# A layer of attention and a mixture of experts on one core: both batches routed in one run, the weight marks on ScalarE, the second half turned inside the first

## The chip, the core and the metric

The kernel runs on one core of a Trainium2 chip. A core has four compute engines with a queue each: TensorE (PE; its weight loads are listed as PEld), VectorE (DVE), ScalarE (ACT) and GpSimd (POOL); SyncE (SP) only issues transfers. The engines run on their own and meet at semaphores. All of them work from SBUF, an on-chip memory of 128 partitions; TensorE writes to PSUM. The metric is the time of the whole program on the device in microseconds; less is better. All times are from the profile of one execution or from the runs in the table below.

## What is computed

The input is 2 batches of 2048 tokens of 256 numbers. First comes attention with 16 heads of 16, added to the input and normalised; then every token goes to its two likeliest of 8 experts, the result is added and normalised again:

```
x = layernorm(x + attention(x))
probs = softmax(x @ router_weight.T)              # 4096 tokens x 8 experts
topk_probs, selected = top_k(probs, 2); weights divided by their sum
# each expert takes at most 1280 tokens, the heaviest weights first
expert_inputs[e, slot] = x[token]
expert_out = (pre * silu(gate)) @ post            # pre, gate: 256 -> 1024, post: 1024 -> 256
out[token] = sum over its kept slots of weight * expert_out
x = layernorm(x + out)
```

In this data no expert is over its 1280 places, so slots may be given in token order; the other case is in the code behind a branch and is not taken.

## The kernel before

The program is three blocks with a barrier of all engines between them. The first makes the projections and the second the attention, up to 1094 us of the span. The third holds the rest, and the change lies in it alone.

**Normalising and logits.** Tokens lie 128 to a tile, 32 tiles (`TT`), 16 (`NT`) to a batch. `measure_h(b)` on VectorE turns the row statistics of a batch into mean and scale: seven small instructions in `layer_stats` (L153 to L159), a root on ScalarE (L1289), six more. Then groups of 4 tiles are normalised in `x_sb` by VectorE and ScalarE, turned by TensorE (L1136), multiplied by the router's weights (L1144), copied by ScalarE (L1312) and turned back (L1151) into the logits `lg_ps[b]`; there are 8 groups, 4 a batch. SyncE stores the normalised rows to DRAM twice, as `h_dram` (what experts gather) and as `acc_dram` (what results are added to).

**Routing.** `route(b)` on VectorE is a chain of about 50 instructions over 16 tiles x 8 experts (128 elements): softmax (with an Exp on ScalarE, L1305), the two picks, weights, then a running count per expert (`prefixes`, from two products on TensorE, L1119 and L1120) and the place of each choice (`places`), split into a partition `at_p` and a column `at_q` of the slot table. Batch 1 adds the totals of batch 0. Each instruction waits for the one before.

**The slot table** `list_ps` (80 columns of token numbers, 80 of weights) is a sum of products. A piece `n` is one choice `k` of 8 tiles; there are 8 pieces. For a piece VectorE makes `in_q` (L1469), `in_p` (L1470) and the number marks (L1474), GpSimd makes the weight marks from `in_q` and `kept_w` (L1036), and TensorE adds up 8 fp32 products (L1160, 16 instructions). `in_q`, `in_p` and `marks` have two buffers each, so piece n+2 waits for the products of piece n (`list_ready`). VectorE copies the table out (L1598, L1599).

**Experts.** GpSimd gathers the rows of an expert from `h_dram` with ten indirect transfers: four for the first half of its slots (`xin_loaded`), six for the second half and the spare tiles (`xrest_loaded`). `turn(j, g)` on TensorE (L1194, 8 instructions) turns half `g` of 512 slots into `xt_ps`; ScalarE and VectorE copy it as a high and a low part (`turn_hi` L1276, `turn_lo` L1613; `xt_split` counts two for each half). An expert's body then has, for each half `g`, eight steps `f` of `up` (12 products of 128x512, L1202), each followed by a gate on ScalarE (L1374), the product `mid` (L1687), and its high (L1377) and low part (L1616); then eight steps of `down` (12 products of 128x256, L1210). `up(f)` waits for the `mid` of f-2. `split_down` parts the second weight matrix (high part on GpSimd L1027, low part on VectorE L1607, at `f == 4` of half 0), `split_up` the first (ScalarE L1285, VectorE L1512). Experts 0 to 5 are a loop of three rounds of two; a spare third part of 256 slots is computed only where an expert has over 1024 tokens (three of the eight). In the second half's `down` steps TensorE turns both halves of the next expert, at f = 0 and f = 4; before expert 0 both are turned as soon as their gathers have landed.

At the start of the third block GpSimd clears `y` and `xin` of both buffers (L1021, L1022: 128x2560 each), then parts expert 0's second matrix (L1027), which SyncE has loaded.

## Time and profile before

| | us |
|---|---|
| median of 3 runs (lowest, highest) | 1867.17 (1865.07, 1868.34) |
| the profiled execution: its own time | 1867.23 |
| the profiled execution: span of the trace | 1865.3 |

| stretch of the span | us |
|---|---|
| projections and attention | 0 to 1094 |
| normalising and logits | 1094 to 1148 |
| routing and slot table (overlaps the logits of batch 1) | 1138 to 1209 |
| gathering and turning for expert 0 | 1209 to 1228 |
| the eight experts | 1228 to 1834 |
| last rows out | 1834 to 1865 |

TensorE is busy in 89% of the span, ScalarE in 68%, VectorE in 64%, GpSimd in 17%. These are averages over stages that have little in common: in the stretch from 1094 to 1228 us TensorE is mostly idle, in the experts it is nearly always at work. The views used below are the page's slices (the span in 40 equal parts), the instructions in order of time, the chain of waits (what released what, back from the end), the busy time by stretch, and the groups of instructions by form.

### The profile page before, as it was taken

To read this page: it belongs to the slowest core of one execution; us is meant where nothing else is said; L and a number is where in the kernel's file an instruction comes from. 1 tells how busy PE (TensorE), PEld (TensorE's weight loads), DVE (VectorE), ACT (ScalarE), POOL (GpSimd) and SP (SyncE) were. 2 spreads that over 40 slices of the span, in tenths; PEclk is the share of its full clock that TensorE was granted. 3 is DMA by queue.
4 is the path that set the end of the run, shared out by engine and by line. 5 is a ranking of instruction groups with operands and counts; after the bars stand their busy time and mean duration, and the time that the engine had idled before them with its cause. 6 is when DMAs were issued, how large, how long until landed. Compare 5 with 4: busy or idle time off the path is not lost. (4 is left out here: it accounts for less than half of the span.)

```text
span 1865.3 us, 31730 instructions
## 1 busy us (share of the span) xinstructions
PE 1658.0 (89%) x10822; PEld 1016.4 (54%) x10823; DVE 1193.3 (64%) x2238; ACT 1271.8 (68%) x1422; POOL 323.0 (17%) x306
## 2 busy tenths in 40 slices
PE   7949999999999999999999956379989998999995
PEld 6713333333333333333333323368978997889985
DVE  6846868676777768686877766834444553545564
ACT  7739999999999999999999953023333342433433
POOL 0000000000000000000000021243424424344154
PEclk9969999999999999999999978779999999999998
DMA  5561010101010100101010005122222313323143
GB/s 176 170 183 47 30 29 23 32 19 34 17 34 17 34 24 27 28 23 32 20 34 17 17 23 180 46 68 63 61 59 60 102 14 103 68 58 101 13 124 112
DMA packets 74746, 108.27 MB, mean 58 GB/s; under 512 B 10778, under 2 KB 59715, under 8 KB 74672
## 3 DMA queue, kind: packets, MB, share of 16 engines
q1 hardware_dynamic: 59792, 89.42, 15.1%
q0 software_dynamic: 14880, 17.82, 5.5%
q8 instruction: 51, 0.84, 0.2%
q14 instruction: 23, 0.19, 0.0%
HBM read 75.77 MB, written 35.91 MB: 60 GB/s over the span
## 5 line engine op out<-in xcount | busy, mean ns | idle before, releaser
L690 ACT ACTIVATE probs<-scores 128x1536 f32<-128x1536 f32 (+1 forms) x384 | 520.6, 1379 | 42.8 <-PE scores L620 37.5
L733 DVE TENSOR_REDUCE sums<-expq 128x1 f32<-128x1408 f32 (+6 forms) x448 | 347.4, 828 | 13.0 <-ACT expq L696 13.0
L620 PE MATMUL scores<-aq,ak 98*128 98x512 bf16 (+3 forms) x1280 | 304.0, 352 | 56.9 <-DMA aq<-shift_dram 22.0
L636 PE MATMUL o_ps<-probs,vh 128*32 128x512 f32 (+3 forms) x2560 | 339.1, 542 | 0.0
L1374 ACT ACTIVATE gate<-up_ps 128x512 f32<-128x512 f32 x128 | 76.5, 598 | 327.2 <-PE up_ps L1202 327.2
L620 PE MATMUL scores<-ak,aq 98*128 98x512 bf16 (+3 forms) x1184 | 263.8, 342 | 17.0 <-ACT probs L690 9.0
L696 ACT ACTIVATE expq<-scores 128x1536 f32<-128x1536 f32 x192 | 274.7, 1449 | 2.0
L720 DVE TENSOR_TENSOR hidden<-probs,after 128x384 f32<-128x384 f32 x128 | 70.9, 554 | 238.9 <-ACT probs L690 238.9
L620 PEld LDWEIGHTS scores<-aq,ak 98*128 98x128 bf16 x1280 | 96.6, 98 | 230.2 <-ACT probs L690 73.2
L620 PEld LDWEIGHTS scores<-ak,aq 98*128 98x128 bf16 x1184 | 91.0, 98 | 238.5 <-ACT expq L696 94.7
L1202 PE MATMUL up_ps<-xeT_hi,wup_hi 128*128 128x512 f32 x512 | 203.1, 397 | 18.3 <-issue 13.5
L1687 DVE TENSOR_TENSOR mid<-up_ps,gate 128x512 f32<-128x512 f32 x128 | 88.3, 691 | 194.7 <-ACT gate L1374 192.1
L1202 PE MATMUL up_ps<-xeT_hi,wup_lo 128*128 128x512 f32 x512 | 201.6, 394 | 0.0
L1202 PE MATMUL up_ps<-xeT_lo,wup_hi 128*128 128x512 f32 x512 | 201.4, 393 | 0.0
L699 ACT ACTIVATE scores<-scores 128x1536 f32<-128x1536 f32 x128 | 185.5, 1450 | 0.0
L1210 PE MATMUL y_ps<-w_hi,mid_hi 128*128 128x256 f32 x560 | 157.3, 281 | 0.0
L1210 PE MATMUL y_ps<-w_lo,mid_hi 128*128 128x256 f32 x560 | 156.2, 279 | 0.0
L1210 PE MATMUL y_ps<-w_hi,mid_lo 128*128 128x256 f32 x560 | 156.0, 279 | 0.0
L577 POOL COPY vh<-v_all 128x256 f32 (+1 forms) x32 | 12.6, 396 | 727.5 <-PE o_ps L636 724.4
L1094 POOL DMA_INDIRECT acc_dram<-y,row x70 | 109.2, 1559 | 136.7 <-DVE y L1648 90.6
L1202 PEld LDWEIGHTS up_ps<-xeT_hi,wup_hi 128*128 128x128 f32 x512 | 97.8, 191 | 39.7 <-issue 16.0
L636 PEld LDWEIGHTS o_ps<-probs,vh 128*32 128x32 f32 x2560 | 50.8, 108 | 123.8 <-issue 98.4
(241 smaller groups left out, 2607.7 us busy)
## 6 DMA issues: line engine op xcount, KB each, us to landing
raw<-w_T SPq DMA_DIRECT2D x16, 1024.0 KB, 7.4
split_dram<-parts SPq DMA_DIRECT2D x48, 256.0 KB, 2.9
aq<-split_dram SPq DMA_DIRECT2D x192, 64.0 KB
raw<-wg_T SPq DMA_DIRECT2D x8, 1024.0 KB, 4.9
ak<-split_dram SPq DMA_DIRECT2D x32, 192.0 KB
xT<-x_T SPq DMA_DIRECT2D x8, 512.0 KB, 4.9
ak<-split_dram SPq DMA_DIRECT2D x32, 128.0 KB
x_sb<-x_tok SPq DMA_DIRECT2D x1, 4096.0 KB, 25.2
```

What stands on the lines that cost most here:

```text
L620: last = nc.tensor.matmul(dst[:, at:at + w], still, moving[0:KS, lo:lo + w], start=True, stop=True, skip_group_check=True)
L636: last = nc.tensor.matmul(dst[32 * r:32 * r + 32, BLK - w:BLK], vh[j % 2][:, k, :], probs[:, m % P_RING, at:at + w], start=first, stop=Tru ...
L690: last = nc.scalar.activation(probs[:, m % P_RING, 0:w], src[:, 0:w], ACT.Exp, scale=HD ** -0.5)
L696: last = nc.scalar.activation(expq[:, n % X_RING, 0:w], src[:, 0:w], ACT.Exp, scale=HD ** -0.5)
L699: last = nc.scalar.activation(src[:, at:at + w], src[:, at:at + w], ACT.Exp, scale=HD ** -0.5, accum_out=sums[:, j, col:col + 1])
L720: nc.vector.tensor_tensor(hidden[:, 0:3, :], three, after[:, 0:3, :], ALU.mult).then_inc(hidden_ready, 1)
L733: last = nc.vector.tensor_reduce(sums[:, j % 2, col:col + 1], expq[:, n % X_RING, at:at + w], AX.X, ALU.add)
L1094: pool.indirect_dma_start(out=acc_dram[:, :], out_offset=bass.IndirectOffsetOnAxis(ap=row[j][:, t:t + 1], axis=0), in_=y[j][:, t, :], in_o ...
L1202: last = nc.tensor.matmul(up_ps[n % 2][:, k, 0:cols.stop - cols.start], wup[a][:, k, c, f * P:(f + 1) * P], x[b][:, c, cols], start=(c == ...
L1210: last = nc.tensor.matmul(y_ps[:, t, :], mid2[a][:, f, t * P:(t + 1) * P], w2[b][:, f, :], start=(f == 0 and t % 2 == 0 and (a, b) == PAIR ...
L1374: nc.scalar.activation(gate[f % 2][:], up_ps[f % 2][:, 0, :], ACT.Silu).then_inc(silu_done, 1)
L1687: nc.vector.tensor_tensor(mid[f % 2][:], up_ps[f % 2][:, 1, :], gate[f % 2][:], ALU.mult).then_inc(mul_done, 1)
```

## The change

1. `route()` handles all 32 tiles in one run (256 elements an instruction); only the first two instructions stay per batch. One Exp on ScalarE takes both batches. The prefix products are one pair of 256 columns.
2. `split_up(0, 0)` stands before `route()`; it was between the marks of batch 0 and the routing of batch 1. The eight pieces follow in one row, ordered by tiles and then choice. The instructions on totals (L1530 to L1539 before) stand once before them, as they did before the last four.
3. The weight marks are made by ScalarE, in 8 instructions of 128x80 a piece, not by GpSimd in one of 128x640.
4. GpSimd clears only the spare part of each `y` (two instructions of 128x512).
5. Half 1 of an expert is turned inside half 0 of the same expert, before the `up` of f = 4, for expert 0 too. `split_down` moves from f = 4 to f = 5 on VectorE.

VectorE around the first stretch of routing. `wup_lo` is the low part of expert 0's first matrix, `red` and `work` are the first two steps of the routing, `rprobs` the output of the Exp. Before:

```order
L1416 TENSOR_SCALAR x_sb<-x_sb,mean,rstd 128x256 x8
L1481 TENSOR_REDUCE red<-xt_ps 128x16
L1482 TENSOR_TENSOR work<-xt_ps,red 128x128
L1485 TENSOR_REDUCE red<-rprobs 128x16
L1486 RECIPROCAL tmp<-red 128x16
```

Now:

```order
L1410 TENSOR_SCALAR x_sb<-x_sb,mean,rstd 128x256 x8
L1503 TENSOR_TENSOR wup_lo<-raw,wup_hi 128x1024 x4
L1476 TENSOR_REDUCE red<-xt_ps 128x16
L1477 TENSOR_TENSOR work<-xt_ps,red 128x128
L1476 TENSOR_REDUCE red<-xt_ps 128x16
L1477 TENSOR_TENSOR work<-xt_ps,red 128x128
L1481 TENSOR_REDUCE red<-rprobs 128x32
```

The four `wup_lo` moved ahead of the routing, and the chain behind the Exp waits for the logits of both batches.

ScalarE from the last groups of logits to the first expert. `hT` and `lT` are its copies in the logits, `xeT_hi` the high part of a turned half. Before:

```order
L1294 ACTIVATE x_sb<-x_sb,nbias,rstd 128x256 x2
L1301 ACTIVATE hT<-up_ps 128x512 x2
L1312 ACTIVATE lT<-up_ps 8x512
L1305 ACT_TABLE_LOAD
L1305 ACTIVATE rprobs<-work 128x128
L1301 ACTIVATE hT<-up_ps 128x512 x2
L1312 ACTIVATE lT<-up_ps 8x512 x2
L1305 ACTIVATE rprobs<-work 128x128
L1276 ACTIVATE xeT_hi<-xt_ps 128x512 x4
```

Now:

```order
L1282 ACTIVATE x_sb<-x_sb,nbias,rstd 128x256 x2
L1289 ACTIVATE hT<-up_ps 128x512 x2
L1305 ACTIVATE lT<-up_ps 8x512
L1289 ACTIVATE hT<-up_ps 128x512 x2
L1305 ACTIVATE lT<-up_ps 8x512 x2
L1322 ACT_TABLE_LOAD
L1322 ACTIVATE rprobs<-work 128x256
L1297 ACTIVATE marks<-in_q,kept_w 128x80 x64
L1264 ACTIVATE xeT_hi<-xt_ps 128x512 x2
```

The table load for the Exp stands behind the last copy of logits, 64 marks are new, and two of the four copies of the turned rows have gone from here.

TensorE from the end of the slot table to expert 0. Before:

```order
L1160 MATMUL y_ps<-marks,in_p 128x160 x64
L1178 UNCONDITIONAL_BRANCH
L1194 MATMUL xt_ps<-ident,xin 128x128 x16
L957 UNCONDITIONAL_BRANCH
L957 ISA
L966 TENSOR_LOAD more
```

Now, first the same place and then, behind the line of three dots, the fourth and fifth `up` of half 0:

```order
L1153 MATMUL y_ps<-marks,in_p 128x160 x64
L1170 UNCONDITIONAL_BRANCH
L1186 MATMUL xt_ps<-ident,xin 128x128 x8
L958 UNCONDITIONAL_BRANCH
...
L1194 MATMUL up_ps<-xeT_lo,wup_hi 128x512
L1230 ISA
L1186 MATMUL xt_ps<-ident,xin 128x128 x8
L1233 REGISTER_ALU
L1194 MATMUL up_ps<-xeT_hi,wup_hi 128x512
```

Eight of the sixteen turning instructions went from ahead of expert 0 to the middle of its first half.

```diff
-        PIECES = [(b, k, half) for b in range(B) for half in range(2) for k in range(TOPK)]
+        PIECES = [(k, part) for part in range(TT // OHP) for k in range(TOPK)]
+        TURN_AT_F = 4
...
                 for j in range(2):
-                    pool.memset(y[j][:], 0.0).then_inc(y_cleared, 1)
-                    pool.memset(xin[j][:], 0.0).then_inc(y_cleared, 1)
+                    pool.memset(y[j][:, 2 * NA:CT, :], 0.0).then_inc(y_cleared, 1)
...
-                for n in range(NP):
-                    k, tiles = of_piece(n)
-                    pool.wait_ge(eq_ready, n + 1)
-                    if n >= 2:
-                        pool.wait_ge(list_ready, n - 1)
-                    nc.gpsimd.tensor_tensor(marks[n % 2][:, :, 1, :], in_q[n % 2][:], wide(kept_w[:, k, tiles], NSLOT), ALU.mult).then_inc(wgt_ready, 1)
...
-                        pe.wait_ge(wgt_ready, n + 1)
+                        pe.wait_ge(wgt_ready, OHP * (n + 1))
...
-                for b in range(B):
-                    pe.wait_ge(keep_ready, b + 1)
-                    prefix_products(of_batch(b)).then_inc(prefix_ready, 1)
-                    for n in range(b * NP // B, (b + 1) * NP // B):
-                        list_piece(n, 0)
+                pe.wait_ge(keep_ready, 1)
+                prefix_products(ALL).then_inc(prefix_ready, 1)
+                for n in range(NP):
+                    list_piece(n, 0)
...
                 pe.wait_ge(xin_loaded[0], 16 * NA)
-                for g in range(2):
-                    if g == 1:
-                        pe.wait_ge(xrest_loaded[0], 16 * (CT - NA))
-                        pe.wait_ge(xt_split, DC)
-                    turn(0, g)
+                turn(0, 0)
...
-                    pe.wait_ge(xt_split, count(4, i, j, 4))
+                    pe.wait_ge(xt_split, count(4, i, j, 2))
...
                         for f in range(FC):
+                            if g == 0 and f == TURN_AT_F:
+                                pe.wait_ge(xrest_loaded[j], i * (16 * (CT - NA)) + 16 * (CT - NA))
+                                turn(j, 1)
...
                         if g == 0:
+                            pe.wait_ge(xt_split, count(4, i, j, 4))
...
-                            if g == 1 and prep and f == FC // 2:
-                                pe.wait_ge(xrest_loaded[1 - j], i * (16 * (CT - NA)) + 16 * (CT - NA) * (j + 1))
-                                pe.wait_ge(xt_split, count(2 * DC, i, j, 3 * DC))
-                                turn(1 - j, 1)
...
-                def exponentials(b):
-                    act.wait_ge(logit_off, b + 1)
-                    nc.scalar.activation(probs[:, of_batch(b), :], work[:, of_batch(b), :], ACT.Exp).then_inc(p_exp, 1)
+                def weights(n):
+                    k, tiles = of_piece(n)
+                    act.wait_ge(eq_ready, n + 1)
+                    if n >= 2:
+                        act.wait_ge(list_ready, n - 1)
+                    for t in range(OHP):
+                        nc.scalar.activation(marks[n % 2][:, t, 1, :], in_q[n % 2][:, t, :], ACT.Copy,
+                                             scale=kept_w[:, k, tiles.start + t:tiles.start + t + 1]).then_inc(wgt_ready, 1)
...
-                route(0)
-                for n in range(NP // B):
-                    mark(n, 0)
                 split_up(0, 0)
-                route(1)
+                route()
...
-                for n in range(NP // B, NP):
+                dve.wait_ge(places_ready, 1)
+                for n in range(NP):
                     mark(n, 0)
...
-                            if g == 0 and f == FC // 2:
+                            if g == 0 and f == TURN_AT_F:
+                                turn_lo(i, j, 1)
+                            if g == 0 and f == TURN_AT_F + 1:
                                 split_down(i, j)
...
                         if g == 1 and prep:
                             turn_lo(i, j + 1, 0)
                             split_up(i, j + 1)
-                            turn_lo(i, j + 1, 1)
```

## Rows read from the trace of the kernel before

**Rows 1.** Chain of waits, 1095 to 1106 us: start, duration, what.

```profile
1095.85 8.97 DVE var L158
1104.84 1.82 DVE var L159
```

**Rows 2.** GpSimd in order of time: start, duration, what.

```profile
1096.04 2.23 POOL L1021 MEMSET y<- 128x2560 f32 x1
...
1104.73 1.88 POOL L1027 CAST w_hi<-raw 128x2048 fp32r<-128x2048 f32 x1
```

**Rows 3.** By stretch: length, busy us of each engine, clock, DMA share, GB/s.

```profile
1100.00:1101.00 1.00, 0.00 (x0) 0.00 (x0) 1.00 (x1) 0.00 (x0) 1.00 (x2) 0.50 0.05 14
```

**Rows 4.** TensorE and ScalarE in order of time, the end of the logits.

```profile
1147.54 0.41 PE L1151 MATMUL xt_ps<-ident,lT 8*128 8x8 f32 x4 [0.34 <-ACT lT L1312]
...
1141.70 1.28 ACT L1305 ACT_TABLE_LOAD   x1
...
1146.90 0.59 ACT L1312 ACTIVATE lT<-up_ps 8x512 f32<-8x512 f32 x1 [1.57 <-PE up_ps L1144]
```

**Rows 5.** VectorE in order of time, the routing.

```profile
1137.80 0.29 DVE L1481 TENSOR_REDUCE red<-xt_ps 128x16 f32<-128x128 f32 x1 [6.69 <-PE xt_ps L1151]
1143.41 0.28 DVE L1485 TENSOR_REDUCE red<-rprobs 128x16 f32<-128x128 f32 x1 [4.99 <-ACT rprobs L1305]
1155.56 0.83 DVE L1469 TENSOR_TENSOR in_q<-upward,at_q 128x640 f32<-128x640 f32 x1
1171.33 4.62 DVE L1512 TENSOR_TENSOR wup_lo<-raw,wup_hi 128x1024 fp32r<-128x1024 f32 x4
1189.40 0.16 DVE L1530 TENSOR_SCALAR big<-total 1x8 f32<-1x8 f32 x1
1190.89 0.82 DVE L1469 TENSOR_TENSOR in_q<-upward,at_q 128x640 f32<-128x640 f32 x1
1208.90 0.24 DVE L1598 COPY slot_w<-y_ps 128x80 f32<-128x80 f32 x1 [2.75 <-PE y_ps L1160]
```

**Rows 6.** VectorE and GpSimd in order of time, the marks of the first piece.

```profile
1156.30 1.22 DVE L1470 TENSOR_TENSOR in_p<-upward,at_p 128x1024 f32<-128x1024 f32 x1
1157.43 1.88 DVE L1474 TENSOR_TENSOR marks<-in_q,ids 128x640 f32<-128x640 f32 x1
...
1156.47 2.16 POOL L1036 TENSOR_TENSOR marks<-in_q,kept_w 128x640 f32<-128x640 f32 x1 [49.85 <-DVE in_q L1469]
```

**Rows 7.** TensorE: a first piece in the chain of waits; a later one in order of time.

```profile
1159.37 4.59 PE y_ps L1160 x16
...
1206.21 2.44 PE L1160 MATMUL y_ps<-marks,in_p 128*128 128x160 f32 x16 [1.22 <-DVE marks L1474]
```

**Rows 8.** Groups by form on ScalarE: count, busy us, mean ns, idle before.

```profile
L1377 ACT ACTIVATE mid_hi<-mid 128x512 fp32r<-128x512 f32 x128 | 80.3, 627 | 5.3 <-DVE mid L1687 5.3
L1368 ACT ACTIVATE mid_hi<-mid 128x256 fp32r<-128x256 f32 x24 | 9.9, 411 | 0.6 <-DVE mid L1669 0.6
L1294 ACT ACTIVATE x_sb<-x_sb,nbias,rstd 128x256 f32<-128x256 f32 x16 | 8.6, 587 | 2.7 <-DVE nbias L1412 2.7
```

**Rows 9.** TensorE in order of time, before expert 0's first product.

```profile
1217.60 1.97 PE L1194 MATMUL xt_ps<-ident,xin 128*128 128x128 f32 x8 [8.95 <-DMA xin<-h_dram,row]
1224.76 1.97 PE L1194 MATMUL xt_ps<-ident,xin 128*128 128x128 f32 x8 [5.19 <-DMA xin<-h_dram,row]
1228.22 0.79 PE L1202 MATMUL up_ps<-xeT_hi,wup_hi 128*128 128x512 f32 x1 [1.49 <-DVE xeT_lo L1613]
```

**Rows 10.** Chain of waits, expert 0's second half to expert 2's start.

```profile
1263.34 21.77 PE up_ps L1202 x96
...
1291.65 0.87 PE xt_ps L1194 x8
...
1383.08 6.11 issue
```

**Rows 11.** VectorE in order of time, half 0 of expert 7.

```profile
1789.64 2.32 DVE L1607 TENSOR_TENSOR w_lo<-raw,w_hi 128x2048 fp32r<-128x2048 f32 x1
```

More of the change, by code:

```diff
@@ L939, in of_piece @@
             def of_piece(n):
-                b, k, half = PIECES[n]
-                return k, slice(b * NT + half * OHP, b * NT + (half + 1) * OHP)
+                k, part = PIECES[n]
+                return k, slice(part * OHP, (part + 1) * OHP)
             def token_tile(t):
@@ L1327, in _ @@
                         split_up_piece(g - 1)
-                    if g == NGR - 1:
-                        exponentials(0)
-                exponentials(1)
+                act.wait_ge(logit_off, 1)
+                nc.scalar.activation(probs[:], work[:], ACT.Exp).then_inc(p_exp, 1)
+                for n in range(NP):
+                    weights(n)
                 turn_hi(0, 0, 0)
-                turn_hi(0, 0, 1)
                 def root(n):
@@ L1474, in mark, with route @@
                     nc.vector.tensor_tensor(marks[n % 2][:, :, 0, :], in_q[n % 2][:], wide(ids[:, tiles], NSLOT), ALU.mult).then_inc(id_ready, 1)
-                def route(b):
-                    tiles = of_batch(b)
-                    p, w, r = probs[:, tiles, :], work[:, tiles, :], red[:, tiles]
-                    dve.wait_ge(lg_ready, GB * (b + 1))
-                    link(nc.vector.tensor_reduce(r, lg_ps[b][:, 0:NT, :], AX.X, ALU.max))
-                    nc.vector.tensor_tensor(w, lg_ps[b][:, 0:NT, :], wide(r), ALU.subtract).then_inc(logit_off, 1)
+                def route():
+                    tiles = ALL
+                    p, w, r = probs[:], work[:], red[:]
+                    for b in range(B):
+                        dve.wait_ge(lg_ready, GB * (b + 1))
+                        link(nc.vector.tensor_reduce(red[:, of_batch(b)], lg_ps[b][:, 0:NT, :], AX.X, ALU.max))
+                        last = nc.vector.tensor_tensor(work[:, of_batch(b), :], lg_ps[b][:, 0:NT, :], wide(red[:, of_batch(b)]), ALU.subtract)
+                    last.then_inc(logit_off, 1)
                     dve.wait_ge(iota_ready, 8)
-                    dve.wait_ge(p_exp, b + 1)
+                    dve.wait_ge(p_exp, 1)
                     link(nc.vector.tensor_reduce(r, p, AX.X, ALU.add))
@@ L1498, in route @@
                     weigh(link, kept_w, wgt, tiles)
[L1499 to L1504 removed]
+                    upto_tile = prefixes(link, 1, tiles)
+                    link(nc.vector.tensor_copy(total[:], upto_tile[:, TT - 1, :]))
                     places(link, tiles)
[L1506 removed]
                 def split_up(i, j):
@@ L1539, in _ @@
                 nc.vector.tensor_scalar(flag[0:1, 1:2], over[0:1, :], float(CAP), None, ALU.is_gt).then_inc(over_ready, 1)
-                for n in range(NP // B, NP):
+                dve.wait_ge(places_ready, 1)
+                for n in range(NP):
                     mark(n, 0)
@@ L1690, in body @@
                                 lo_of_mid(f - 1, GA).then_inc(mid_split, 1)
-                            if g == 0 and f == FC // 2:
+                            if g == 0 and f == TURN_AT_F:
+                                turn_lo(i, j, 1)
+                            if g == 0 and f == TURN_AT_F + 1:
                                 split_down(i, j)
```

24 lines of the change are left out of this document (8 added, 16 removed).

## The prediction

> **What bounds the kernel now.** I read the slices first, for where TensorE is idle, then the chain of waits over those places, then each engine in order of time there. In the experts the chain is TensorE alone: 12 products an `up` step, 21.77 us a half [rows 10]. Between 1094 and 1228 us it is not. First VectorE stands still: an instruction on 16 numbers (L158) takes 8.97 us and the next 1.82 us [rows 1], while GpSimd clears four buffers and then casts [rows 2]. Then the chain of the routing on VectorE, twice, with the marks of four pieces behind each [rows 5]. Last the gathers for expert 0: its second half is turned 7.16 us after the first, and only then the first product starts [rows 9]. The change touches these three places, and apart from the turning nothing else.
>
> **Start of the block.** L158 begins at 1095.85 and ends when the last clearing does; L159 ends with the cast [rows 1, 2]. That two engines exclude each other there is read from these ends. Now two clearings of 512 remain. At 2.17 us from one start to the next for 2560, or 0.85 ns each, they take about 0.45 us each and are through at 1097.0. L158 would end there and L159 0.2 us later, at 1097.25, where it ended at 1106.65. The cast can't come at once: it needs the second matrix, whose transfer keeps the DMA engines full until just past 1100 (share 0.05 in the next us) [rows 3]. So it runs from about 1100.4 to 1102.3. By then the root and the six small steps behind it are done: they took 3.0 us from the end of L159 before, so until 1100.1 now. What follows, the normalising, works on rows of another form. I take no collision. **Gain 9.4 us.** Bounds: 7.5 if the cast catches a step (it lasts 1.88), 10.5 if L158 waits for no clearing at all.
>
> The Trainium skill (SBUF — State Buffer, section "SBUF: two separate sides") says the pair of ports shared by VectorE and GpSimd is locked for a whole instruction and the loser blocks until that one ends. By the letter of it L158 would have waited for one clearing, not four; the row says four, so I let it wait for both new ones. By the rule the gain would be 0.5 us more.
>
> **The logits.** They keep their pace: TensorE ends them at 1147.95 [rows 4], less the 9.4 us. All times below leave this shift out. The Exp and its table load go from amid ScalarE's copies to behind the last (ends 1147.49) [rows 4]; TensorE was busy meanwhile, so nothing is won. The four `wup_lo`, 4.62 us, go into VectorE's idle 6.69 us before L1481 [rows 5]: their high parts exist by then, so they are free. They were on the path at 1171.33. SyncE waits for them to load expert 1's matrices. That load stands behind the stores of the rows in its queue, so 2 MB now follow these directly, while VectorE still routes and nothing gathers. Free too.
>
> **One routing.** Batch 1's two first steps run from 1148.0 to 1148.6. The table load (1.28 us) carries no wait and starts at 1147.5, so the Exp of 256 runs from 1148.8 for 0.41 us, as a plain form of that size [rows 4, 8]. VectorE goes on at 1149.3. Before, this chain took 1143.41 to 1155.56, 12.15 us, for 16 tiles [rows 5]. 27 of its steps double from 128 to 256 elements. A step of 128 lasts 0.29, one of 640 0.83 [rows 5], so 1.05 ns an element and 0.135 us a step: 3.6 us. The running count needs one doubling more (0.45), small steps grow by 0.3 together. That is 16.5 us, to 1165.8. The totals take 1.49 us (1189.40 to 1190.89) [rows 5] as before: marks start at 1167.3. The prefix product of 256 columns has the 1.9 us of the weights beside it to hide in; a stall there is 0.3 at most.
>
> The Trainium skill (ScalarE: Activation LUTs, section "What ACT_TABLE_LOAD costs") adds a drain to the load, 2.66 us in all. The trace has 1.28 and the load right behind the copy. By the page the Exp would be 1.35 us later and the time 1838.4.
>
> **The marks.** VectorE's number marks take 1.88 us for 640 elements where `in_q`, of the same size, takes 0.83 [rows 5, 6]. GpSimd's product reads the same buffer; it ends at 1158.63, and from there to the mark's end at 1159.31 are 0.68 us, 640 elements at the slope above (0.67): VectorE had waited. Without GpSimd I take 0.82. From start to start `in_q` takes 0.74, `in_p` 1.13, and the mark then 0.75: 2.62 us a piece, over a us less. ScalarE: plain forms of 512 and 256 take 627 and 411 ns, so 0.84 ns an element and 262 ns for 80. The form with two pointer operands takes 587 for 256 [rows 8], so 88 ns a pointer: 350 ns. Back to back such instructions overlap by 0.09 us, so 0.26 each, 2.17 us for the eight. TensorE: 2.44 us a piece; 4.59 for the first behind a pause [rows 7], in which the granted clock is 0.50, the lower level [rows 3].
>
> No engine is the bound, the ring of two buffers is: `in_q` 0.82, marks 2.17, products 2.44 and three handovers of 0.06 make 5.6 us for two pieces. From 1167.3: weight marks of piece 0 at +3.1, its products end at +7.7, those of piece 6 three turns later at +24.5, of piece 7 2.6 behind, at +27.1. The table is copied out from 1194.5, where it was from 1208.90 [rows 5]: **gain 14.4 us**. Of this 4.6 is `wup_lo`; one Exp path, one chain start and the marks are the rest. Bounds: ScalarE at 0.5 each (587 less the overlap) adds 1.85 to three turns and the first piece, 7.4 us less gain. Marks still at 1.88 cost 5.0. The ring bound by VectorE alone and a first piece at 2.44: 3.3 more.
>
> **Turning inside the first half.** From the first turning's end (1219.57) to the first product was 1.49 us behind the second one's end; the same lag now gives 1221.06 instead of 1228.22, 7.16 us earlier [rows 9]. The eight instructions come back in half 0, 0.87 us [rows 10]. For the other experts 0.87 goes from one `down` to the next `up`, zero. The six gathers had landed by 1224.76, and step 4 comes four steps of at least 2.72 us in, at 1231.9: no wait. **Gain 6.3 us.**
>
> ScalarE and VectorE take the copies at f = 4, each engine two. A form of 512 is 0.6 us on ScalarE [rows 8], and 0.7 on VectorE by the slope above. A step gives 2.72 us (21.77 / 8), of which VectorE uses two such forms. Counted from the end of `up(4)`: `mid` until 1.3, low part until 1.9, copies until 3.15, and the next `mid` is wanted at 3.35. In step 5 `split_down`, 2.32 us [rows 11], ends at 6.95 and delays `mid(6)` by 0.8. No `up` waits for that one before the next half; `down` needs it after 8.2. So TensorE doesn't stop; the cover has 0.2 us at f = 4 and, since `up(7)` waits for `mid(5)` only at 5.4, 1.3 behind it.
>
> **Sum.** 9.4 + 14.4 + 6.3 = 30.1 us. The profiled execution took 1867.23 (span 1865.3), the median of the runs is 1867.17, so no correction: 1867.2 - 30.1 = **1837.1**, a span of 1835.2.
>
> **Rivals.**
> *The cast collides*: it waits on its transfer, but should that end 0.4 us earlier, it holds L165 to L1412. 1839.0. For it: only 0.3 us of room [rows 3]. Chance 0.08.
> *ScalarE paces the marks*: small instructions cost 0.5 each, as the 256-wide pair does. 1844.5. Against it: the fit from two sizes. 0.06.
> *VectorE's marks stay at 1.88*: their length is their own, not GpSimd's. 1842.1. Against: the fit of the two ends [rows 6]. 0.04.
> *The copies in step 4 hold the products*: a us an expert, 8 in all, 1845.1. For it: 0.2 us of room. 0.07.
> *The drain* of the table load, 1838.4: 0.03.
> *Slower than before*: TensorE stops in the middle of a half at each turning, as it does for 6.11 us where the expert loop starts over [rows 10], by a late wait or a fetch at the new place. Eight such stops are 49 us, less the 30.1: 1886. It decides from 3.8 us a stop. Against it: the turnings in `down` cost 0.87 each and no more, with waits just as many. 0.03, of which 0.01 lies about the deciding point, no change.
> *Not what it says*: batches are merged, but the gathers wait for another thing, the stores of the rows, and start no earlier; only the 6.3 of the turning are left, 1860.9. Against it: before, GpSimd was waiting for the table [rows 5, 9], not for them. 0.01.
>
> **How the numbers follow.** The forecast holds 0.68, from 1833 to 1840. The range of 1832.5 to 1844 adds the collision, the drain, the marks at 1.88 and the near half of the copies; the low end is the bounds of 1.1 and 3.3 together. A difference under 0.2% can't be told from none here, 3.7 us. Faster by more: 0.97; within: 0.01; slower: 0.02.
>
> **What would show it.** L158 ends near 1097 and L159 lasts 0.2. The Exp starts 0.2 us behind VectorE's last logit step. Number marks take 0.8, weight marks 0.35 each and 2.2 a piece, `in_q` every 2.6 and 3.0 us in turn. The table is ready 23.8 us earlier than before, the first `up` 31.0 earlier, every later one 30.1. I am wrong if an `up` half takes over 22.8 us, if TensorE waits for `mid` or the turned rows inside a half, or if pieces are over 3 us apart.

## The result

| | before | changed |
|---|---|---|
| median of 4 runs (lowest, highest) | 1866.13 (1865.07, 1868.34) | 1839.55 (1839.13, 1840.90) |
| the profiled execution: its own time | 1867.23 | 1839.2 |
| the profiled execution: span | 1865.3 | 1837.5 |

The ratio is 0.9857 (95% interval 0.9845 to 0.9869): the changed kernel is faster by some 27 us. Forecast was 1837.1, so 30.1 us; the span of the profiled execution gave 27.8. One run of the last experiment (2388.38 us, with a mean granted clock of 0.648 where all others have 0.96 or 0.97) is left out of its numbers. From here to the end of this document a stage is measured in the span, from the end of one step to the end of the next, so that the sum can be compared term by term:

| stage | before | changed | gain | forecast |
|---|---|---|---|---|
| attention ends, L153 starts | 1094.75 | 1095.31 | -0.56 | 0 |
| L153's start to L159's end | 11.89 | 2.50 | 9.39 | 9.4 |
| L159's end to the last logit | 41.31 | 40.11 | 1.20 | 0 |
| last logit to the table's copy | 60.95 | 47.65 | 13.30 | 14.4 |
| copy to the first turning | 8.70 | 8.70 | 0.00 | 0 |
| first turning to the first `up` | 10.62 | 3.64 | 6.98 | 7.16 |
| first `up` to the end of the span | 637.08 | 639.59 | -2.51 | -0.87 |
| sum | | | 27.80 | 30.1 |

### The profile page after: what moved, and what is told of

It is laid out like the page before. It is cut to its first block and busy times, and to the rows that moved or that the text cites. A ratio compares the mean times of both kernels' runs of the same rounds, so it can differ in the third digit from the quotient of the medians.

```text
span 1837.5 us, 31725 instructions
## 1 busy us (share of the span) xinstructions
PE 1655.9 (90%) x10818; PEld 1015.6 (55%) x10819; DVE 1170.0 (64%) x2192; ACT 1287.7 (70%) x1485; POOL 296.5 (16%) x296
## 5 line engine op out<-in xcount | busy, mean ns | idle before, releaser
L620 PEld LDWEIGHTS scores<-aq,ak 98*128 98x128 bf16 x1280 | 96.5, 98 | 230.5 <-ACT probs L690 73.2
L577 POOL COPY vh<-v_all 128x256 f32 (+1 forms) x32 | 12.6, 396 | 727.6 <-PE o_ps L636 724.6
```

The costliest lines, as they stand in the source:

```text
L620: last = nc.tensor.matmul(dst[:, at:at + w], still, moving[0:KS, lo:lo + w], start=True, stop=True, skip_group_check=True)
```

## The profile after

**Start of the block.** VectorE and GpSimd in order of time (start, duration, what), the answer to [rows 1, 2]:

```profile
1096.40 1.20 DVE L158 TENSOR_SCALAR var<-var 128x16 f32<-128x16 f32 x1
1097.64 0.17 DVE L159 TENSOR_TENSOR var<-var,tmp 128x16 f32<-128x16 f32 x1
...
1100.65 2.95 DVE L1410 TENSOR_SCALAR x_sb<-x_sb,mean,rstd 128x256 f32<-128x256 f32 x4
1103.98 0.69 DVE L1416 COPY hT<-up_ps 128x512 f32<-128x512 f32 x1 [0.38 <-PE up_ps L1129]
```

```profile
1096.60 0.98 POOL L1022 MEMSET y<- 128x512 f32 x2
1101.57 1.89 POOL L1027 CAST w_hi<-raw 128x2048 fp32r<-128x2048 f32 x1 [3.99 <-DMA raw<-w_T]
```

L158 ends with the second clearing, at 1097.60, and L159 is an ordinary small step again. The cast came at 1101.57, 3.76 us behind L159, and did hold something: VectorE's first four normalisings, of which it met the last, took 2.95 us, where before they took 1.38. It cost nothing, since VectorE's next step waits for TensorE, 0.38 us where it was 1.95. The 1.57 us went out of that cover.

**Exp.** ScalarE and VectorE in order of time, the answer to [rows 4]:

```profile
1136.87 0.59 ACT L1305 ACTIVATE lT<-up_ps 8x512 f32<-8x512 f32 x1 [1.57 <-PE up_ps L1137]
1137.47 1.28 ACT L1322 ACT_TABLE_LOAD   x1
1138.77 0.42 ACT L1322 ACTIVATE rprobs<-work 128x256 f32<-128x256 f32 x1
```

```profile
1138.28 0.29 DVE L1477 TENSOR_TENSOR work<-xt_ps,red 128x128 f32<-128x128 f32 x1
1139.28 0.42 DVE L1481 TENSOR_REDUCE red<-rprobs 128x32 f32<-128x256 f32 x1 [0.71 <-ACT rprobs L1322]
```

The table load runs beside VectorE's last two logit steps; the Exp follows it at once. It starts 0.2 us behind VectorE's end (1138.57), so at most that is paid for the load.

**Marks.** VectorE, ScalarE and TensorE in order of time, the first, third and fourth piece, and the table's copy; the answer to [rows 5 to 7]:

```profile
1157.55 0.80 DVE L1463 TENSOR_TENSOR in_q<-upward,at_q 128x640 f32<-128x640 f32 x1
...
1159.42 0.81 DVE L1468 TENSOR_TENSOR marks<-in_q,ids 128x640 f32<-128x640 f32 x1
...
1165.30 0.83 DVE L1463 TENSOR_TENSOR in_q<-upward,at_q 128x640 f32<-128x640 f32 x1 [2.47 <-PE y_ps L1153]
...
1168.25 0.83 DVE L1463 TENSOR_TENSOR in_q<-upward,at_q 128x640 f32<-128x640 f32 x1 [0.25 <-PE y_ps L1153]
```

```profile
1158.39 2.12 ACT L1297 ACTIVATE marks<-in_q,kept_w 128x80 f32<-128x80 f32 x8 [19.21 <-DVE in_q L1463]
```

```profile
1160.66 7.55 PE L1153 MATMUL y_ps<-marks,in_p 128*128 128x160 f32 x32 [12.49 <-ACT marks L1297]
1168.43 2.41 PE L1153 MATMUL y_ps<-marks,in_p 128*128 128x160 f32 x16 [0.22 <-ACT marks L1297]
```

```profile
1185.57 0.24 DVE L1587 COPY slot_w<-y_ps 128x80 f32<-128x80 f32 x1 [3.46 <-PE y_ps L1153]
```

The group of this line by form, which gives one weight mark its length:

```profile
L1297 ACT ACTIVATE marks<-in_q,kept_w 128x80 f32<-128x80 f32 x64 | 17.0, 348 | 26.2 <-DVE in_q L1463 26.2
```

The number mark takes 0.81 us, a weight mark 348 ns and eight of them 2.12 us. From the third piece on, `in_q` starts 2.95 and 2.63 us apart in turn, each second one behind the products of two pieces ago: the ring of two buffers is the bound, as worked out. From VectorE's first step behind the Exp to the first `in_q` are 18.27 us, 0.3 over the forecast.

**Turning and the experts.** TensorE in order of time, the answer to [rows 9]:

```profile
1194.27 1.97 PE L1186 MATMUL xt_ps<-ident,xin 128*128 128x128 f32 x8 [9.32 <-DMA xin<-h_dram,row]
1197.91 0.79 PE L1194 MATMUL up_ps<-xeT_hi,wup_hi 128*128 128x512 f32 x1 [1.67 <-DVE xeT_lo L1602]
```

and the chain of waits (start, duration, what; x counts instructions) at the start of expert 0 and of expert 2, the answer to [rows 10]:

```profile
1197.91 12.57 PE up_ps L1194 x48
1210.48 0.87 PE xt_ps L1186 x8
1211.36 10.90 PE up_ps L1194 x48
...
1352.43 6.03 issue
1358.46 14.10 PE up_ps L1194 x48
```

The turning costs 0.87 us in the middle of a half and nothing around it. Behind the pause of 6.03 us the first 48 products take 14.10 us, where 48 that follow without a pause take 10.90. By stretch (length, busy us and count of PE, PEld, DVE, ACT, POOL, then PE's clock, DMA share and GB/s), here in the changed kernel, 3.5 to 5.5 us behind that start, and then in the kernel before, 3.8 us behind the start of the same half:

```profile
1362.00:1364.00 2.00, 2.00 (x6) 1.57 (x5) 0.00 (x0) 0.02 (x1) 0.10 (x1) 0.50 0.63 72
```

```profile
1393.00:1395.00 2.00, 2.00 (x11) 1.65 (x10) 0.62 (x1) 0.60 (x1) 0.00 (x0) 1.00 0.55 72
```

In one execution TensorE is still granted 0.50, the lower level of 1.2 GHz, when in the other it has 2.4 GHz. The longer stay at the lower clock is the largest piece that the forecast lacks.

## The experiments

One table first, since all readings come from the same places of each trace: L159's end behind L153's start, the table's copy behind the last logit, the first `up` behind the first turning, and the three `up` halves that follow a pause (of experts 0, 2 and 4; an undisturbed one takes 21.77; the turning is left out). A ratio is to the kernel before as it ran beside that group of kernels: 1866.13 us for the first measurement, 1866.31 for the four in which one part stands alone or is undone, 1867.04 for the next four, 1868.64 for the last two. Medians of different groups are compared by their ratios.

| kernel | L159 | table | first `up` | halves behind a pause | median | ratio to before |
|---|---|---|---|---|---|---|
| before | 11.89 | 60.95 | 10.62 | 23.82, 23.56, 23.55 | | |
| changed | 2.50 | 47.65 | 3.64 | 23.47, 24.99, 24.23 | 1839.55 | 0.9857 |
| only the clearing | 2.51 | 60.46 | 10.61 | 23.73, 23.49, 23.47 | 1856.61 | 0.9952 |
| GpSimd's weight marks | 2.45 | 56.02 | 3.55 | 24.39, 23.90, 24.86 | 1848.47 | 0.9905 |
| turned in `down` | 2.51 | 47.65 | 10.65 | 24.98, 24.24, 23.85 | 1843.60 | 0.9880 |
| two routes | 2.46 | 51.55 | 3.55 | 24.99, 24.19, 23.65 | 1843.71 | 0.9877 |
| changed, again | 2.45 | 47.32 | 3.56 | 24.56, 24.03, 23.79 | 1838.87 | 0.9849 |
| three buffers | 2.45 | 44.00 | 3.63 | 23.65, 23.51, 23.48 | 1834.80 | 0.9831 |
| totals last | 2.51 | 45.84 | 3.55 | 24.46, 23.89, 24.84 | 1837.24 | 0.9839 |
| both of these | 2.51 | 42.95 | 3.63 | 24.98, 24.19, 23.89 | 1833.09 | 0.9819 |
| old clearing, with waits | 3.76 | 60.89 | 10.60 | 23.79, 23.58, 24.79 | 1866.11 | 0.9983 |
| `split_down` at f = 4 | 2.51 | 47.31 | 3.63 | (TensorE stops in them) | 1849.96 | 0.9892 |

### The clearing alone

```diff
-                    pool.memset(y[j][:], 0.0).then_inc(y_cleared, 1)
-                    pool.memset(xin[j][:], 0.0).then_inc(y_cleared, 1)
+                    pool.memset(y[j][:, 2 * NA:CT, :], 0.0).then_inc(y_cleared, 1)
```

> The kernel before with one part of the change alone: GpSimd clears two pieces of 128x512 (the spare part of each y) and no more. My theory: L158 and L159 were only held by GpSimd, so L159 ends 8.8 to 9.4 us earlier, and the clock of the first products of the logits stays up a us more; all that follows moves along: 10 to 10.6 us off the time, 1856. Rival, the cast collides: it lands on the small steps behind the root and takes back up to 1.9 us, 1858. Rival, the start of the block is not on the path (something else, such as the transfers, holds the logits): under 3 us, 1864.

Measured: 1856.61, ratio 0.9952 (0.9935 to 0.9969). L159 ends 9.38 us earlier behind L153 than before, and this kernel has none of the other parts. The term of 9.4 us is this edit's alone.

### The old clearing, with a wait between two

Each clearing but the first now waits for the one before to be finished; nothing else is changed from the kernel before.

```diff
                     pool.memset(y[j][:], 0.0).then_inc(y_cleared, 1)
+                    pool.wait_ge(y_cleared, 2 * j + 1)
                     pool.memset(xin[j][:], 0.0).then_inc(y_cleared, 1)
+                    pool.wait_ge(y_cleared, 2 * j + 2)
```

> The kernel before, with a wait of GpSimd for its own clearing behind each of the four. My theory from L158, which sat through four clearings of 2.2 us, and from the run with GpSimd's marks, whose first one sat through four instructions of VectorE: the engine that has the next instruction at hand keeps the shared way to SBUF, and the other gets in only where it pauses. The waits make such a pause, so L158 ends with the first clearing: L159 ends about 3.7 us behind L153's start where it was 11.9, and the time is some 8 to 9 us less, 1858. Rival, L158 waits for all clearings whatever lies between them: 11.9 and 1867. Rival, between: it gets in behind the first clearing, but L159 or a later small step is caught by the next ones, 2.2 us each time: 6 to 10 and 1861 to 1865.

Measured: 1866.11, ratio 0.9983 (0.9974 to 0.9993). VectorE and then GpSimd in order of time:

```profile
1095.18 2.45 DVE L158 TENSOR_SCALAR var<-var 128x16 f32<-128x16 f32 x1
1097.67 0.18 DVE L159 TENSOR_TENSOR var<-var,tmp 128x16 f32<-128x16 f32 x1
...
1100.17 2.04 DVE L167 TENSOR_SCALAR tmp<-tmp 128x16 f32<-128x16 f32 x1
1102.24 0.18 DVE L168 TENSOR_TENSOR rstd<-rstd,tmp 128x16 f32<-128x16 f32 x1
...
1102.55 4.61 DVE L1418 TENSOR_SCALAR x_sb<-x_sb,mean,rstd 128x256 f32<-128x256 f32 x4
```

```profile
1095.38 2.23 POOL L1021 MEMSET y<- 128x2560 f32 x1
1097.66 2.23 POOL L1023 MEMSET xin<- 128x2560 f32 x1
1099.95 2.23 POOL L1021 MEMSET y<- 128x2560 f32 x1
1102.24 2.23 POOL L1023 MEMSET xin<- 128x2560 f32 x1
```

The same four clearings in the same time: without a wait between them L158 stood 8.97 us, through all four [rows 1, 2]; with one it stood through the first alone and ended 0.02 us behind it. So here GpSimd kept the way as long as its next instruction was at hand. This is no rule for every place: in the slot table the two engines took turns, as the next experiment shows. The time of 1858 was missed, and the rival in between is the nearer one: L159 ends 8.13 us earlier, but L167 waits out the third clearing, and the normalising, held by the fourth and then by the cast, takes 4.61 us instead of 1.38, more than its cover of 1.95. Of the 8.13 us 4.2 are left at the first `up`. Behind it this execution is 2.1 us longer, 1.2 of them in the three halves behind a pause.

The lines also show who is held. L159, L168 and L164 to L166 (not shown; each 0.17 to 0.25 us) run inside a clearing. L158, L167 and L1418 don't. The ones held are all of the form TENSOR_SCALAR, with one tensor read; the ones let through beside a clearing read two, or are a reciprocal. Beside the cast, which reads as well as writes, L159 with two tensors was held too [rows 1, 2].

The Trainium skill (SBUF — State Buffer, section "SBUF: two separate sides") has this split: held are VectorE's two-port modes, and its instructions with two inputs only against a GpSimd instruction that reads. The three kinds of line agree with it. What it says of the length, one whole instruction, agrees with this run (2.45 us) and not with the kernel before (8.97 us).

### The weight marks back on GpSimd

```diff
+                for n in range(NP):
+                    k, tiles = of_piece(n)
+                    pool.wait_ge(eq_ready, n + 1)
+                    if n >= 2:
+                        pool.wait_ge(list_ready, n - 1)
+                    nc.gpsimd.tensor_tensor(marks[n % 2][:, :, 1, :], in_q[n % 2][:], wide(kept_w[:, k, tiles], NSLOT), ALU.mult).then_inc(wgt_ready, 1)
...
-                for n in range(NP):
-                    weights(n)
```

> The changed kernel with one part undone: GpSimd makes the weight marks again, one instruction of 128x640 a piece. My theory: the number marks on VectorE grow from 0.82 back to 1.88 us, because GpSimd reads the same buffers at that time, and a piece takes 3.67 us of VectorE, which becomes the bound in place of the ring of two buffers: the table is copied out about 4 us later than in the changed kernel (eight pieces, 7 x 0.88 less what the slow first piece hides), 1843.5. Rival, the length of the marks is their own in that place: they stay at 0.82 with the ring about as long, since GpSimd's 2.17 us equals ScalarE's 2.12: no difference to the changed kernel, 1839.5.

Measured: 1848.47, ratio 0.9905 (0.9889 to 0.9922), a table 8.37 us later than in the changed kernel, not the 4 that were expected. VectorE in order of time, then GpSimd, then all eight of GpSimd's products (shortest, median and longest in ns):

```profile
1161.66 0.81 DVE L1473 TENSOR_TENSOR marks<-in_q,ids 128x640 f32<-128x640 f32 x1
1168.37 0.83 DVE L1468 TENSOR_TENSOR in_q<-upward,at_q 128x640 f32<-128x640 f32 x1 [5.91 <-PE y_ps L1160]
1169.11 1.22 DVE L1469 TENSOR_TENSOR in_p<-upward,at_p 128x1024 f32<-128x1024 f32 x1
1170.25 1.88 DVE L1473 TENSOR_TENSOR marks<-in_q,ids 128x640 f32<-128x640 f32 x1
1172.05 0.81 DVE L1468 TENSOR_TENSOR in_q<-upward,at_q 128x640 f32<-128x640 f32 x1
```

```profile
1158.07 6.72 POOL L1036 TENSOR_TENSOR marks<-in_q,kept_w 128x640 f32<-128x640 f32 x2 [55.18 <-DVE in_q L1468]
1169.28 2.17 POOL L1036 TENSOR_TENSOR marks<-in_q,kept_w 128x640 f32<-128x640 f32 x1 [4.48 <-DVE in_q L1468]
```

```profile
L1036 POOL TENSOR_TENSOR marks<-in_q,kept_w x8: 1251/2171/5512, 1158.1 to 1187.6; 128x640 f32<-128x640 f32 x8
```

From the third piece on it is as in the kernel before: GpSimd's product takes 2.17 us and VectorE's mark 1.88, it ends 0.68 us behind GpSimd's, and pieces come 3.68 us apart. That a mark alone takes 0.81 is shown both by this and by the changed kernel, and the rival of a length of its own falls. GpSimd's 2.17 us are no length of its own either: the shortest, 1.25 us, is the second product, which followed the first at about 1163.6 while VectorE stood idle. Beside VectorE the two engines take turns. GpSimd's product waits some 0.9 us for `in_p` (1169.11 to 1170.33) and then runs for 1.25; the number mark waits 1.06 us for it and then runs for 0.82. In the kernel before it was the same [rows 6], in all eight pieces. From the third `in_q` to the copy this costs 4.93 us of the 8.37.

The other 3.44 lie in the first two pieces, where it went the other way round: VectorE's marks took 0.81, and the chain of waits has GpSimd's first product from 1158.07 for 5.52 us, until 1.12 us after VectorE stopped at 1162.47, about the time that the product takes alone. Here VectorE, with its instructions on end, kept the way, through `in_p` and four more. Why it kept it in this piece and gave it up behind `in_p` in the kernel before, where both engines started in the same order 0.17 us apart [rows 6], no run tells. It stays open.

### Both halves turned ahead, the rest of the change kept

```diff
+                pe.wait_ge(xrest_loaded[0], 16 * (CT - NA))
+                pe.wait_ge(xt_split, DC)
+                turn(0, 1)
...
-                            if g == 0 and f == TURN_AT_F:
-                                pe.wait_ge(xrest_loaded[j], i * (16 * (CT - NA)) + 16 * (CT - NA))
-                                turn(j, 1)
...
+                            if g == 1 and prep and f == FC // 2:
...
+                                turn(1 - j, 1)
```

> The changed kernel with one part undone: both halves of an expert are turned as before, in the down steps of the expert ahead, and both of expert 0 before its first product. My theory: the first product of expert 0 starts 7.0 us later, a turning of 0.87 us leaves its first half, so 6.2 us more at expert 1; the place of the turning costs the loop nothing else: 1845.7. Rival, the move itself costs something in the loop: the halves behind the restart of the loop (expert 2 and 4) took 24.99 and 24.23 us with the turning in them where 23.56 + 0.87 and 23.55 + 0.87 would be 24.4. If the move is the cause of the longer low clock there, the two fall back to 23.6 each in this kernel and the time is 1845. If they scatter alike from run to run with the turning in either place, it is not the move.

Measured: 1843.60, ratio 0.9880 (0.9864 to 0.9897). The first `up` comes 10.65 us behind the first turning instead of 3.64: 7.01, of which 0.87 returns in half 0. The time is 2 us under what was expected; the execution with the profile came to L153 2.1 us earlier than the changed kernel's, which accounts for it there (the other three have no profile). Its halves behind a pause are as long as those of the changed kernel, 24.98, 24.24 and 23.85, though nothing is turned inside them: the longer halves are not the moved turning's doing.

### Two routes, the rest kept

The routing runs per batch again, with the four pieces of batch 0 between; `split_up(0, 0)` stays ahead, the marks stay on ScalarE.

```diff
-                route()
+                route(0)
+                for n in range(NP // B):
+                    mark(n, 0)
+                route(1)
...
-                for n in range(NP):
+                for n in range(NP // B, NP):
                     mark(n, 0)
```

> The changed kernel with the merging undone: batch 0 is routed and its four pieces marked, then batch 1, with the Exp of batch 0 amid the logits again. The early low part of expert 0's matrix, ScalarE's marks and the rest stay as changed. My theory: the chain for 16 tiles takes 12.2 us twice where one of 32 took 16.8, the first starts 4.5 us before the last logits, the ring runs up twice and the table products start behind a pause twice. Worked out from the rows: batch 0's chain starts at 1132.7 (1143.41 less the shift of 10.7 or so) and ends at 1144.9, its pieces take 3.1 + 4.6 + 2 x 2.8 = about 11 to VectorE's last mark, batch 1's chain with its 0.6 of logits, its Exp and totals 15 us, its four pieces 16 to the copy: 1187. That is 1.5 us later than in the changed kernel: 1841. Rival, merging is most of the gain: it drops one whole chain of 12 us: 1847 and more. Rival, merging gives nothing or costs, because batch 0's chain hides partly in the logits: 1838 or less.

Measured: 1843.71, ratio 0.9877 (0.9860 to 0.9893). VectorE in order of time, the first marks of batch 0 and the start of batch 1's route:

```profile
1145.95 0.82 DVE L1471 TENSOR_TENSOR in_q<-upward,at_q 128x640 f32<-128x640 f32 x1
...
1158.94 0.28 DVE L1483 TENSOR_REDUCE red<-xt_ps 128x16 f32<-128x128 f32 x1
```

Behind the last logit the table is copied at 51.55 instead of 47.65, so merging is worth 3.9 us there, and 4.5 behind L153's start, of which 0.7 lies in the logits, where the kernels scatter by more. Expected were 1.5: batch 0's pieces take VectorE from 1145.95 to 1158.94, 13 us and not about 11, while batch 1's logits lie ready since 1138. Of the 13.3 us, `wup_lo` is 4.6 by its row [rows 5], the merging 3.9, and what is left for the marks is 4.8. The first and the last of these have no run of their own: undoing the marks alone cost 8.37, so the parts don't simply add.

### The changed kernel again

> The changed kernel as it is, once more, as the neighbour of the three that follow. My theory of the 2 us by which the first measurement missed: the time at the lower clock behind each pause of TensorE scatters from execution to execution. The three halves behind a pause (experts 0, 2 and 4) took 23.47, 24.99 and 24.23 us there; here they take other values between 23.4 and 25. Stages without a pause repeat to 0.1 us: table 47.65 us behind the logits, first product 12.34 behind the table. Rival: they repeat too, and 24.99 and 24.23 belong to this program. Time 1839.5.

Measured: 1838.87, ratio 0.9849 (0.9832 to 0.9865), in line with the first measurement. The three halves did take other values, 24.56, 24.03 and 23.79, with the same code. That the other stages repeat to 0.1 us did not hold. The table came 47.32 us behind the logits, 0.33 earlier, since the second piece's products took 2.4 us and not 3.2. The logits themselves took 41.14 us, where the first measurement had 40.11: TensorE's logits of the fourth group, just behind its wait of 4.53 us, took 3.58 us, where they had taken 2.33.

```profile
1121.29 3.58 PE L1137 MATMUL up_ps<-hT,wr 128*8 128x512 f32 x4
```

### A third buffer

`in_q`, `in_p` and `marks` get a third buffer, laid over `y`, which isn't in use yet. Only the waits' distance changes.

```diff
-                    if at >= 2:
-                        dve.wait_ge(list_ready, at - 1)
+                    if at >= RING:
+                        dve.wait_ge(list_ready, at - RING + 1)
```

> The changed kernel with three buffers instead of two for in_q, in_p and marks (the third lies in the y buffers, which are idle then). My theory, the ring of two is the bound: VectorE goes on every 2.62 us without a wait, TensorE's products stand nearly back to back, and the table is copied out 2.3 us earlier (45.3 behind the logits, where it was 47.65): 1837.3. Rival, the supply is the bound: VectorE or ScalarE pace the pieces anyway, at most 0.3 us: 1839.3. Rival, the slow first piece is all: TensorE's 8 pieces are a row of their own behind it and gain 1 us: 1838.5.

Measured: 1834.80, ratio 0.9831 (0.9814 to 0.9847), 4.1 us under the changed kernel beside it. The table is 3.65 us earlier than in the changed kernel's first profile and 3.32 than in its second; expected were 2.3. TensorE in order of time:

```profile
1176.04 2.41 PE L1158 MATMUL y_ps<-marks,in_p 128*128 128x160 f32 x16 [0.20 <-ACT marks L1303]
1178.64 2.41 PE L1158 MATMUL y_ps<-marks,in_p 128*128 128x160 f32 x16 [0.19 <-ACT marks L1303]
```

The products follow each other at 2.60 us, the time in which VectorE makes its three tensors of a piece without a wait. That the ring, and no engine, set the pace is shown; now VectorE sets it, and TensorE has 0.2 us to spare. In this execution the pauses were followed by 23.65, 23.51 and 23.48 us. In the chain of waits, at expert 2:

```profile
1348.81 5.89 issue
1354.71 12.62 PE up_ps L1199 x48
```

The same products with the same turning behind `up(3)` and the same pause took 12.62 us here and 14.10 in the changed kernel, which itself took 13.14 when it ran again. So 1 us at least of the extra time is the execution's and not the code's; with one profile a kernel, nothing tells more.

### The totals behind the marks, and both together

The eleven small steps of the totals (L1518 to L1527 in the changed kernel) go behind the last mark, where VectorE waits for the products anyway.

```diff
+                dve.wait_ge(places_ready, 1)
+                for n in range(NP):
+                    mark(n, 0)
                 link(nc.vector.tensor_scalar(big[0][:], total[0:1, :], float(2 * GA)
...
-                dve.wait_ge(places_ready, 1)
-                for n in range(NP):
-                    mark(n, 0)
```

> The changed kernel with the eleven small instructions on the totals behind the last mark instead of ahead of the first. My theory: they cost 1.49 us of the path ahead of the marks and nothing behind them, where VectorE waits 3.46 us for TensorE: 1.5 us earlier, the table 46.2 behind the logits: 1838. Rival: the branch that needs them (too many rows for an expert) now resolves later on every engine and gives the 1.5 us back: 1839.5.

> The changed kernel with both: three buffers, and the totals behind the last mark. My theory: the gains add, table 43.8 us behind the logits, 3.8 us off the changed kernel: 1835.7. Rival, with three buffers VectorE has less slack behind its last mark, so the totals show again: 1837.

Measured: 1837.24, ratio 0.9839 (0.9823 to 0.9855), a table 1.48 us earlier than in the changed kernel's second profile; the steps had cost 1.47 (1156.08 to 1157.55). With both edits 1833.09, ratio 0.9819 (0.9802 to 0.9835), a table 4.37 us earlier than in that profile, a little less than 3.32 and 1.48 together. Beside the changed kernel on the same chip, 1838.87, that is 5.8 us less: the fastest kernel of this study.

### `split_down` in the step of the copies

To see how much cover the copies of the turned rows have, VectorE's 2.28 us of `split_down` go from step 5 back to step 4, behind them.

```diff
-                            if g == 0 and f == TURN_AT_F + 1:
                                 split_down(i, j)
```

> The changed kernel with split_down put back to f = 4, so that VectorE does the turned rows' low parts (1.28 us) and the low part of the second matrix (2.3 us) in the same step. My theory, by the slack worked out in the prediction: mid(5), wanted 3.35 us behind the end of up(4), starts at 5.4 and ends at 6.1, and up(7) wants it at 5.44: TensorE stops 0.7 us in each of the eight first halves, 5.5 us in all: 1845. Rival, the slack is larger than worked out and nothing is lost: 1839.3. Rival, the loss spreads to the down steps: over 1.5 us an expert, 1852.

Measured: 1849.96, ratio 0.9892 (0.9872 to 0.9912), against 0.985 for the changed kernel, so some 7 us more. VectorE and then TensorE in order of time, expert 1:

```profile
1289.33 1.28 DVE L1602 TENSOR_TENSOR xeT_lo<-xt_ps,xeT_hi 128x512 fp32r<-128x512 f32 x2
1290.53 2.28 DVE L1596 TENSOR_TENSOR w_lo<-raw,w_hi 128x2048 fp32r<-128x2048 f32 x1
1292.72 0.68 DVE L1675 TENSOR_TENSOR mid<-up_ps,gate 128x512 f32<-128x512 f32 x1
```

```profile
1293.46 0.50 PE L1194 MATMUL up_ps<-xeT_hi,wup_hi 128*128 128x512 f32 x1 [0.57 <-DVE mid L1675]
```

`mid(5)` starts 1.9 us later, and `up(7)`, which waits for it, stops. By the waits of TensorE, over the experts (us in total, times, longest), here and then in the changed kernel:

```profile
PE up_ps L1194 <- DVE mid L1675: 10.0, 10, 3.4
```

```profile
PE up_ps L1194 <- DVE mid L1675: 3.3, 1, 3.3
```

The one wait of the changed kernel lies in the second half of expert 7, where VectorE first does the statistics of the last normalising; the kernel before has it as well (3.4 us). So in the changed kernel no turning makes TensorE wait, and the place of `split_down` is what secures it.

Not all of the other nine waits are the edit's. One of 1.96 us stands ahead of `up(5)` of expert 0, and it begins with ScalarE, before any `split_down`:

```profile
1217.23 0.60 ACT L1367 ACTIVATE gate<-up_ps 128x512 f32<-128x512 f32 x1 [4.57 <-PE up_ps L1194]
```

The products that this gate reads had ended at 1213.02; what kept ScalarE is not in the profile. The other eight, one in each first half ahead of `up(7)`, are 0.24 to 1.04 us long, mostly 0.57. A first half that isn't behind a pause is 0.87 to 0.92 us longer than in the changed kernel: the stop, and the first products behind it, which stand less close. Eight of them make some 7 us, where 5.5 were expected. From the first `up` to the end this profile is 9.3 us longer (648.85 against 639.59); the rest of that is expert 0's late gate.

## Why the prediction was right, and where it was off

**The start of the block** gave 9.39 of 9.4, and for the stated reason: L158 ends with the last clearing of an unbroken row. The run with waits between them shows this, and it was the place where the trace and a rule of one whole instruction stood against each other. The edit alone gave 9.38.

**"I take no collision"** was wrong as a step. The cast began 1.2 us later than I took (1101.57, not 1100.4) and caught the normalising, which I had set aside as rows of another form. The form holds: it is TENSOR_SCALAR, as L158 is. It cost nothing only because VectorE had 1.95 us of cover there.

**The logits** were taken at their old pace and gained 1.20 us in this profile. TensorE had stood for 9.69 us ahead of them, not 19.08, and had the full clock earlier: the first four products of L1137 took 1.88 us, where the same four (L1144 then) took 2.64, and a later four 2.33 where 2.99. Only the first of these is kept when the same kernel runs again (1.88 us). The later four then took 3.58, and the stage 41.14 against 41.31, a gain of 0.17. So most of the 1.20 was the luck of one execution, and it hid a part of what the other terms lacked.

**The routing and the marks** gave 13.30 of 14.4. The chain was 0.27 longer. The first piece's products ended 7.7 us behind the first `in_q`, as forecast, but those of the second took 3.2 us, not 2.44; from there the odd pieces came 2.95 us behind the even ones, not 2.6, and the last product ended at +27.4, not +27.1. The table's copy started 0.62 us behind it, where I had taken 0.1 (and the handover before was 0.25). These three, 0.27, 0.3 and 0.5, make up the 1.1. Marks 0.81, weight marks 348 ns, 2.12 for eight, `in_q` every 2.95 and 2.63: as forecast (0.82, 350, 2.17, 3.0 and 2.6). The drain of the table load, a rival of 0.03, isn't there: the Exp follows 0.02 us behind the load.

**The turning** gave 6.98 of 7.16 (the lag behind the turning was 1.67 us, not 1.49), and took its 0.87 in half 0 as forecast. `mid(6)` of expert 0 was delayed by 0.7 us (1220.89, 0.72 behind its gate), forecast 0.8. No product waited that had not waited before.

**The term that was mis-sized** is the time of the experts. I wrote that every later `up` comes 30.1 us earlier; the halves of experts 2 and 4, behind their pauses, took 24.99 and 24.23 us, together 2.1 more than before, while expert 0's took 0.35 less; the stage as a whole lacks 1.64. This scatters from execution to execution. The same kernel has 24.99 and 24.03 for expert 2 in two profiles, and its last half of expert 7, behind the wait of 3.3 us, was 1.3 us longer in the second. Over the first eleven kernels of the table the three halves sum to 70.6 to 73.2 us, with the turning inside them or not. The kernel before was near the low end in its profiled execution. A forecast from one profile should have carried 1 to 2 us of this in its middle and not only in its range. The other 0.56 us lie ahead of the change: attention ended that much later, and over the kernels L153 starts at 1093.2 to 1095.8.

## What to carry to other kernels

An instruction of 16 numbers that takes 9 us is not slow, it is shut out: look at what the other engine runs in an unbroken row, and shorten the row or move it before any other work on the chain. Then look at which forms are next in that place, since one that is freed of a wait comes earlier and can meet the next long instruction. Where two engines hand pieces to and fro, write down one turn of the ring: here a third buffer in memory that wasn't in use yet gave 3.3 to 3.7 us, where taking GpSimd out of the marks had given 4.8 to 8.4. And before a gain of 1 us is put down to an edit, measure the same kernel twice.

## What the runs showed of the hardware

- GpSimd kept VectorE out over four clearings on end (8.97 us), and over one when a semaphore wait stood between them (2.45 us). VectorE once kept GpSimd out over five of its own (a product that takes 1.25 us beside an idle VectorE took 5.52). In all pieces of the kernel before, and from the third piece on in this one, the two took turns, and the same product took 2.17 us.
- Held beside a clearing were TENSOR_SCALAR forms of 16 and of 256 elements; the two-tensor forms and the reciprocal passed.
- Behind a pause of 6 us TensorE's first 48 products took 14.1 us in one execution of the changed kernel and 13.1 in another, and 12.6 in a kernel with the same experts, with the granted clock at 0.50 for longer or shorter. What decides it is open.
